# Self attention of a decoder layer: score matmuls of two heads in the two halves of the array's rows, units of eight heads, row sums on VectorE, and all loops written out

## The chip, the cores and the metric

The kernel runs on one core of a Trainium2 chip. The metric is the device time of one launch in microseconds. Engines are named as in the profile: PE is TensorE (PEld its weight loads), DVE is VectorE, ACT is ScalarE, POOL is GpSimd, SP is the queue that issues most DMAs.

## The reference

One decoder layer on x of 32 batches x 128 tokens x 128 channels. Only its first part matters for the change:

```python
xn = layernorm(layernorm(x), ln_w, ln_b)
q, k, v = (einsum('bsd,hde->bshe', xn, W) + b for W, b in ...)   # 16 heads of 64
scores = einsum('bqhe,bkhe->bhqk', q, k) / 8, causal mask
z = einsum('bhqk,bkhe->bqhe', softmax(scores), v)
x = x + einsum('bqhe,hed->bqd', z, W_o) + b_o
x = x + cross_attention(layernorm(x), context)                  # 16 heads of 8
x = x + mixture_of_experts(layernorm(x))                        # 8 experts, top 2
```

## The kernel before

The kernel has three stages, one after the other: self attention over the 32 batches, cross attention over the 32 batches, and the experts over eight groups of four batches. The last two batches of self attention are interleaved with the beginning of cross attention (`run_joined`). Each engine has a program of its own, in which the order of the work is written out by hand, and engines meet only in semaphores. An engine takes its instructions strictly in the order written.

**Units and steps.** In self attention `body(b, parity, valid, steps)` is one batch, and its four steps g = 0..3 (`G1`) each begin the scores of one unit of four heads (`HPG`). Work of several batches is in flight: in the body of batch b, step g holds the scores of unit g of batch b, the transposes of unit g-2, the products with the values (z) of unit g-3 (both may belong to batch b-1; `back` works that out), the output projection of batch b-1 (step 3), the Q, K and V projections of batch b+1 (steps 0, 1, 2) and the layer norm of batch b+2.

**One unit.** PE writes the causal mask into a bank of `ps` (a 128x512 matmul with `ident_b`) and adds the scores of four heads. For this `qz` holds the queries of each head over all 128 rows, with zeros in the 64 rows that belong to the other head of the pair, so that every score matmul uses the whole array. DVE takes the row maxima (L640). ACT makes the exponentials, 128 columns at a time because each head has its own bias, and has each instruction give the row sum too (`accum_out`, L536). DVE inverts the sums (L646), POOL multiplies `probs` by them (L390), PE transposes the four blocks (L994), ACT copies the bank to `probsT` (L531), PE multiplies by the values in two halves of the array's columns, and ACT copies that to `zT` (L526). Scores use banks 0 and 1 in turn, transposes banks 2 and 3, z bank 6, projections banks 4 and 5, and bank 7 serves the layer norm's transpose and the output.

**The other work of DVE in a body.** Step 0: queries from the bank to `qz` (L657, four instructions of 64 partitions, two halves of the projection by two heads of a pair) and statistics of the first norm (L681, L684). Step 1: keys to `kT` (L662, two instructions), the first norm (L675) and statistics of the second. Step 2: the second norm `xn` (L687), which waits for POOL's `rstd` (L400). Step 3: `xT` from the bank (L634) and the residual (L693). Matmuls that go through the helper `mm` all bear line 944.

**Loops.** `run_batches` writes out the first bodies, up to batch 2, loops over two bodies at a time (`Fori`), and writes out the last ones. Cross attention does the same, the experts loop over their groups.

Of the kernel before, what the change touches and what calls it, by code (L numbers as in the profile page):

```python
# [19 lines left out]
ALU = mybir.AluOpType  # L20
# [3 lines left out]
P = 128  # L24
# [7 lines left out]
E2 = D // H  # L32
G2 = 8
# [40 lines left out]
def run_batches(eng, first, last, body, steps, after={}):  # L74

    for b in range(first, 3):  # L80
        peel(body, b, steps)
        if b in after:
            after[b]()
    with eng.Fori(3, NB - 3, 2) as i:
        body(i, 1, lambda k: True, steps)
        body(i + 1, 0, lambda k: True, steps)
    for b in range(NB - 3, last):
        peel(body, b, steps)
# [17 lines left out]
def build(nc, x, ctx, W_q, W_k, W_v, W_o, b_q, b_k, b_v, b_o, ln_w, ln_b, w_qkv, w_proj, b_proj,  # L106
          gate_w, gate_proj_w, up_proj_w, down_proj_w, out):
    es = ExitStack()
    with es:
# [51 lines left out]
        qz = sb("qz", [P, 2, PAIRS, 2, P])  # L161
# [55 lines left out]
        raw_gu = qz[:, :, :, :, :].rearrange("p a t c q -> p (a t c) q")  # L217
# [18 lines left out]
        q_rows_zeroed = sem("q_rows_zeroed"); values_zeroed = sem("values_zeroed")  # L236
# [16 lines left out]
        sa_inverse_sums = sem("sa_inverse_sums")  # L253
# [46 lines left out]
        def _(sp):  # L300
# [25 lines left out]
            sp.wait_ge(sa_z_in_bank, G1 * NB)  # L326
# [11 lines left out]
            with sp.Fori(1, NC) as c:  # L338

                sp.wait_ge(expert_added, NE * c + NE)  # L340
                sp.dma_start(out_r[:, bass.ds(CB * c, CB), :], x_all[:, bass.ds(CB * c, CB), :]).then_inc(stored, 16)
# [3 lines left out]
        def _(pool):  # L345
# [154 lines left out]
            with pool.Fori(1, NC) as c:  # L500
                experts(c, False)
# [3 lines left out]
        def _(act):  # L505
# [12 lines left out]
            def self_attention(b, parity, valid, steps):  # L518
                for g in steps:
                    off, u, _ = back(b, parity, g, 3, G1)  # L520
                    if valid(off):
                        t = G1 * (b + off) + u
                        act.wait_ge(sa_z_in_bank, t + 1)
                        if u == 0 and valid(off - 1):
                            act.wait_ge(sa_output, b + off)
                        nc.scalar.copy(zT[:, 2 * u:2 * u + 2, :], ps[6][:, 0:2 * P]).then_inc(sa_z_taken, 1)  # L526
                    off, u, _ = back(b, parity, g, 2, G1)
                    if valid(off):
                        t = G1 * (b + off) + u
                        act.wait_ge(sa_pT_in_bank, t + 1)  # L530
                        nc.scalar.copy(probsT[:, u % 2, :], ps[2 + u % 2][:, :]).then_inc(sa_pT_taken, 1)  # L531
                    if valid(0):
                        t = G1 * b + g
                        act.wait_ge(sa_max, t + 1)
                        for i in range(HPG):
                            last = nc.scalar.activation(probs[:, g, i * P:(i + 1) * P],  # L536
                                                        ps[g % 2][:, i * P:(i + 1) * P], ACT.Exp,
                                                        bias=nmax[:, g, i:i + 1],
                                                        accum_out=rsum[:, g, i:i + 1])
                        last.then_inc(sa_exp, 1)  # L540
                    if g == 2 and valid(1):
# [74 lines left out]
            with act.Fori(1, NC) as c:  # L616
                experts(c, False)
# [3 lines left out]
        def _(dve):  # L621
            nc.vector.memset(qz[:, :, :, :, :], 0.0).then_inc(q_rows_zeroed, 1)

# [4 lines left out]
            def self_attention(b, parity, valid, steps):  # L628
                for g in steps:
# [7 lines left out]
                    if valid(0):  # L637
                        t = G1 * b + g
                        dve.wait_ge(sa_scores, t + 1)
                        nc.vector.reduce_max(nmax[:, g, :], ps[g % 2][:, :].rearrange("p (h k) -> p h k", h=HPG),  # L640
                                             AX_X, negate=True).then_inc(sa_max, 1)
                    off, u, _ = back(b, parity, g, 1, G1)
                    if valid(off):
                        t = G1 * (b + off) + u
                        dve.wait_ge(sa_exp, t + 1)
                        nc.vector.reciprocal(rinv[:, u, :], rsum[:, u, :]).then_inc(sa_inverse_sums, 1)  # L646

                    if valid(1) and g < 2:
                        n, np_ = b + 1, (parity + 1) % 2
                        for half in range(2):  # L650
# [3 lines left out]
                            if g == 0:  # L654
                                for a in range(2):
                                    r = slice(64 * a, 64 * a + 64)
                                    last = nc.vector.scalar_tensor_tensor(  # L657
                                        out=qz[r, np_, own, a, :], in0=tiles[r],
                                        scalar=E1 ** -0.5 / (X1_SCALE * W_SCALE), in1=bcast(bq[r, own], P),
                                        op0=ALU.mult, op1=ALU.add)  # L660
# [35 lines left out]
            def prepare():  # L696
# [6 lines left out]
                dve.wait_ge(q_rows_zeroed, 1)  # L703
# [232 lines left out]
            with dve.Fori(1, NC) as c:  # L936
                experts(c, False)
# [4 lines left out]
        def _(pe):  # L942
# [3 lines left out]
            def self_attention(b, parity, valid, steps):  # L946
                for g in steps:
# [5 lines left out]
                    if g == 2 and valid(0) and not valid(-1):  # L953

                        pe.wait_ge(raw_s_taken, 3)
                        pe.wait_ge(quad_weights_ready, 8)
                        pe.wait_ge(bo_ready, 1)
                    if valid(0):

                        t = G1 * b + g  # L960
                        if g == 0:
                            pe.wait_ge(sa_qk_taken, 4 * b + 4)
                        if g >= 2 or valid(-1):
                            pe.wait_ge(sa_exp, t - 1)
                        bank = ps[g % 2]
                        mm(bank[:, :], ident_b[:, :], causal[:, :, :].rearrange("p h k -> p (h k)"), True, False)
                        for i in range(HPG):
                            h = HPG * g + i
                            last = mm(bank[:, i * P:(i + 1) * P], qz[:, parity, h // 2, h % 2, :],
                                      kT[:, parity, h // 2, :], False, i == HPG - 1)  # L970
# [299 lines left out]
```

## Time and profile before

| | us |
|---|---|
| median of 3 runs | 1299.23 |
| lowest, highest | 1298.95, 1302.72 |
| profiled execution, span from first to last instruction | 1296.2 |
| self attention, first to last causal mask on PE | 26.94 to 531.75 |
| cross attention alone, about | 544 to 1000 |
| experts, about | 1030 to 1296 |

The page gives for the profiled execution its span alone, 1296.2 us; the time of a run also holds what lies before the first and after the last instruction, so the two differ by 3.0 us. Over the whole span PE is busy for 94%, DVE 74%, ACT 69%, POOL 35%. The stages have different limits, so these shares have to be read by stretch: within self attention PE shows 94.6%, DVE 62%, ACT 64%. A body of self attention takes 16.1 us in the trace.

### The profile page before, as it was taken

To read this page: it belongs to the slowest core of one execution; us is meant where nothing else is said; L and a number is where in the kernel's file an instruction comes from. 1 tells how busy PE (TensorE), PEld (TensorE's weight loads), DVE (VectorE), ACT (ScalarE), POOL (GpSimd) and SP (SyncE) were. 2 spreads that over 40 slices of the span, in tenths; PEclk is the share of its full clock that TensorE was granted. 3 is DMA by queue.
4 is the path that set the end of the run, shared out by engine and by line. 5 is a ranking of instruction groups with operands and counts; after the bars stand their busy time and mean duration, and the time that the engine had idled before them with its cause. 6 is when DMAs were issued, how large, how long until landed. Compare 5 with 4: busy or idle time off the path is not lost.

```text
span 1296.2 us, 35573 instructions
## 1 busy us (share of the span) xinstructions
PE 1218.0 (94%) x11851; PEld 932.5 (72%) x11851; DVE 954.3 (74%) x2179; ACT 895.0 (69%) x2950; POOL 448.7 (35%) x796
## 2 busy tenths in 40 slices
PE   5999999999999999899999999999998699999997
PEld 3788888888888778777777777777776366665565
DVE  6666666666666665488888888888886778888887
ACT  2666666666666666698888888888886465555554
POOL 3444444444444444322323333232331342222222
PEclk9999999999999999999999999999999799999999
DMA  6000000000000000000000000000030000000000
GB/s 151 2 2 0 0 0 0 0 0 0 0 0 0 0 0 2 5 14 10 8 12 8 8 11 10 8 8 12 8 102 2 1 10 9 8 8 8 8 8 9
DMA packets 20558, 14.59 MB, mean 11 GB/s; under 512 B 7042, under 2 KB 18596, under 8 KB 20516
## 3 DMA queue, kind: packets, MB, share of 16 engines
q1 hardware_dynamic: 20176, 13.90, 3.9%
q8 instruction: 25, 0.41, 0.1%
q10 hardware_dynamic: 340, 0.14, 0.0%
q14 instruction: 17, 0.14, 0.0%
HBM read 11.94 MB, written 2.10 MB: 11 GB/s over the span
## 4 chain that ended last, share of the span: by engine, by line
PE 47%; issue 23%; DVE 20%; ACT 5%; POOL 3%; DVEq 1%; DMA 1%; POOLq 0%; SPq 0%; ACTq 0%
PE ps L944 35%; PE ps L1088 6%; DVE qz L657 4%; ACT probs L563 3%; PE ps L994 3%; DVE kT L662 3%; DVE xn L687 2%; DVE nmax L785 2%; DVE bst L681 1%; POOL rstd L400 1%; DVE x_all L910 1%; DVE wk L923 1%; POOL h_lo L494 1%; DMA wv<-in_L_attn_W_v 1%; PE ps L952 1%
## 5 line engine op out<-in xcount | busy, mean ns | idle before, releaser
L563 ACT ACTIVATE probs<-ps,nmax 128x256 f32<-128x256 f32 x512 | 238.7, 477 | 13.3 <-DVE nmax L785 11.3
L536 ACT ACTIVATE probs<-ps,nmax 128x128 f32<-128x128 f32 x512 | 183.3, 385 | 28.2 <-DVE nmax L640 28.0
L785 DVE TENSOR_REDUCE nmax<-ps 128x2 f32<-128x512 f32 x256 | 175.3, 685 | 35.3 <-PE ps L944 34.5
L390 POOL TENSOR_TENSOR probs<-probs,rinv 128x512 f32<-128x512 f32 x128 | 133.1, 1040 | 124.7 <-DVE rinv L646 124.7
L944 PE MATMUL ps<-probsT,vm 128*32 128x128 f32 x2048 | 161.5, 279 | 0.0
L1088 PE MATMUL ps<-ident,probs 128*128 128x128 f32 x1024 | 154.5, 273 | 1.2 <-ACT probs L563 1.1
L554 ACT COPY probsT<-ps 128x512 f32<-128x512 f32 x224 | 131.9, 589 | 28.5 <-PE ps L1088 28.1
L526 ACT COPY zT<-ps 128x256 f32<-128x256 f32 x128 | 48.6, 380 | 147.3 <-PE ps L944 147.1
L494 POOL TENSOR_TENSOR h_lo<-wk,h_hi 128x512 f16<-128x512 f32 x64 | 74.0, 1156 | 189.0 <-ACT h_hi L611 186.1
L944 PEld LDWEIGHTS ps<-kT,qz 128*128 128x128 f32 x1024 | 134.5, 192 | 4.0
L944 PE MATMUL ps<-kT,qz 128*128 128x128 f32 x1024 | 134.9, 275 | 0.0
L603 ACT ACTIVATE wq<-ps 128x512 f32<-128x512 f32 x128 | 76.6, 598 | 72.6 <-PE ps L944 72.4
L640 DVE TENSOR_REDUCE nmax<-ps 128x4 f32<-128x512 f32 x128 | 88.3, 690 | 48.0 <-PE ps L944 46.9
L944 PEld LDWEIGHTS ps<-probsT,vm 128*32 128x32 f32 x2048 | 92.8, 109 | 42.7 <-issue 42.5
L1088 PEld LDWEIGHTS ps<-ident,probs 128*128 128x128 f32 x1024 | 118.4, 141 | 7.1 <-ACT probs L563 2.1
L536 ACT ACTIVATION_READ_ACCUMULATOR probs<-ps,nmax 128x1 f32 x512 | 114.3, 223 | 0.0
L928 DVE TENSOR_TENSOR h_lo<-wk,h_hi 128x512 f16<-128x512 f32 x64 | 76.0, 1188 | 43.8 <-ACT h_hi L611 43.8
L611 ACT CAST h_hi<-wk 128x512 f16<-128x512 f32 x128 | 74.3, 617 | 48.7 <-PE ps L944 32.0
L563 ACT ACTIVATION_READ_ACCUMULATOR probs<-ps,nmax 128x1 f32 x512 | 105.3, 206 | 0.0
L944 PE MATMUL ps<-kT,qm 128*128 128x256 f16 x512 | 98.5, 274 | 6.4 <-ACT probs L563 4.3
L944 PE MATMUL ps<-xnT_hi,w_hi 128*128 (+1 forms) x256 | 99.1, 387 | 4.2 <-DVE wk L923 2.4
L657 DVE SCALAR_TENSOR_TENSOR qz<-ps,bq 64x512 f32<-64x512 f32 x128 | 88.1, 688 | 15.4 <-PE ps L944 13.6
(196 smaller groups left out, 3048.7 us busy)
## 6 DMA issues: line engine op xcount, KB each, us to landing
ctx_row<-in_ctx SPq DMA_DIRECT2D x32, 128.0 KB, 2.1
out_x<-x_all SPq DMA_DIRECT2D x8, 256.0 KB, 2.3
kT<-in_L_ffn_down_proj_w SPq DMA_DIRECT2D x1, 1024.0 KB, 10.8
wq<-in_L_attn_W_q SPq DMA_DIRECT2D x1, 512.0 KB, 5.0
wk<-in_L_attn_W_k SPq DMA_DIRECT2D x1, 512.0 KB, 10.1
wv<-in_L_attn_W_v SPq DMA_DIRECT2D x1, 512.0 KB, 10.4
wo<-in_L_attn_W_o SPq DMA_DIRECT2D x2, 256.0 KB, 6.0
x_all<-in_x SPq DMA_DIRECT2D x1, 256.0 KB, 3.0
```

Source lines behind the costliest of these rows:

```text
L390: nc.gpsimd.tensor_tensor(pr, pr, bcast(rinv[:, u, :], P), ALU.mult).then_inc(sa_probs, 1)
L494: nc.gpsimd.tensor_tensor(h_lo[:, e % 2, 0, :], hT[:, 0, :], h_hi[:, e % 2, 0, :], ALU.subtract).then_inc(hidden_low_first, 1)
L536: last = nc.scalar.activation(probs[:, g, i * P:(i + 1) * P], ps[g % 2][:, i * P:(i + 1) * P], ACT.Exp, bias=nmax[:, g, i:i + 1], accum_ou ...
L554: nc.scalar.copy(probsT[:, u % 4, :], ps[2 + u % 2][:, :]).then_inc(ca_pT_taken_act, 1)
L563: last = nc.scalar.activation(probs[:, g % 4, i * KEYS2:(i + 1) * KEYS2], ps[SCORE_BANKS2[g]][:, i * KEYS2:(i + 1) * KEYS2], ACT.Exp, bias ...
L603: nc.scalar.activation(silu[:, i, :], ps[i][:, :], ACT.Silu, scale=1.0 / (NORM_SCALE * W_SCALE)).then_inc(silu_ready, 1)
L640: nc.vector.reduce_max(nmax[:, g, :], ps[g % 2][:, :].rearrange("p (h k) -> p h k", h=HPG), AX_X, negate=True).then_inc(sa_max, 1)
L657: last = nc.vector.scalar_tensor_tensor(out=qz[r, np_, own, a, :], in0=tiles[r], scalar=E1 ** -0.5 / (X1_SCALE * W_SCALE), in1=bcast(bq[r, ...
L785: nc.vector.reduce_max(nmax[:, g, 0:2], ps[SCORE_BANKS2[g]][:, :].rearrange("p (h k) -> p h k", h=2), AX_X, negate=True).then_inc(ca_max, 1)
L928: nc.vector.tensor_tensor(h_lo[:, e % 2, 1, :], hT[:, 1, :], h_hi[:, e % 2, 1, :], ALU.subtract).then_inc(hidden_low_second, 1)
L944: return nc.tensor.matmul(o, l, r, start=start, stop=stop, **kw)
L1088: last = nc.tensor.transpose(ps[2 + u % 2][:, i * P:(i + 1) * P], probs[:, u % 4, i * P:(i + 1) * P], ident[:, :])
```

## The change

It does the following, in self attention except where stated:

- The queries are no longer spread over `qz` with zeros. `qT` holds a pair of heads over 128 partitions, as `kT` does, and is written by two DVE instructions of 128 partitions instead of four of 64. The memset of `qz` goes.
- A score matmul uses the 64 rows of its head, for queries and keys. The two heads of a pair go to the two halves of the array's rows and to two different banks. PE issues the scores of eight heads at once (`HALVES`), in step 0 into banks 0 and 1 and in step 1 into banks 2 and 3, with two mask matmuls ahead of each.
- The softmax units stay at four heads (even or odd ones of eight). Their exponentials no longer give row sums. DVE adds up each unit's `probs` (`reduce_sum`, 128x512 in SBUF), waits for its own semaphore, and inverts.
- z of batch b-1 is made in step 2 of batch b, two halves of eight heads one after the other, in banks 0 and 1, after the exponentials of units 0 and 1 of batch b have read them. ACT copies each half (128x512) to `zT` after the exponentials of unit 2, and after these it takes the transposes of unit 0.
- All transposes go to bank 6, so each unit's transposes wait for ACT's copy of the one before. `probsT` has four buffers in use.
- All `Fori` loops, of cross attention and of the experts too, are written out.

The diff, with the removed loops of the other engines and the declarations left out:

```diff
@@ -81,10 +82,7 @@
-    with eng.Fori(3, NB - 3, 2) as i:
-        body(i, 1, lambda k: True, steps)
-        body(i + 1, 0, lambda k: True, steps)
-    for b in range(NB - 3, last):
+    for b in range(3, last):
...
@@ -158,7 +156,8 @@
-        qz = sb("qz", [P, 2, PAIRS, 2, P])
+        raw_gu = sb("raw_gu", [P, 2 * NE * HT, P])
+        qT = raw_gu[:, 0:2 * PAIRS, :].rearrange("p (a t) q -> p a t q", a=2)
...
@@ -335,10 +333,10 @@
-            with sp.Fori(1, NC) as c:
+            for c in range(1, NC):
-                sp.dma_start(out_r[:, bass.ds(CB * c, CB), :], x_all[:, bass.ds(CB * c, CB), :]).then_inc(stored, 16)
+                sp.dma_start(out_r[:, CB * c:CB * c + CB, :], x_all[:, CB * c:CB * c + CB, :]).then_inc(stored, 16)
...
@@ -516,28 +514,31 @@
                 nc.scalar.activation(w1_hi[:, i, :, :], w[:, :, :], ACT.Copy, scale=W_SCALE).then_inc(w1_high_ready, 1)
 
             def self_attention(b, parity, valid, steps):
-                for g in steps:
-                    off, u, _ = back(b, parity, g, 3, G1)
-                    if valid(off):
-                        t = G1 * (b + off) + u
-                        act.wait_ge(sa_z_in_bank, t + 1)
-                        if u == 0 and valid(off - 1):
-                            act.wait_ge(sa_output, b + off)
-                        nc.scalar.copy(zT[:, 2 * u:2 * u + 2, :], ps[6][:, 0:2 * P]).then_inc(sa_z_taken, 1)
+                def copy_transposed(g):
                     off, u, _ = back(b, parity, g, 2, G1)
                     if valid(off):
-                        t = G1 * (b + off) + u
-                        act.wait_ge(sa_pT_in_bank, t + 1)
-                        nc.scalar.copy(probsT[:, u % 2, :], ps[2 + u % 2][:, :]).then_inc(sa_pT_taken, 1)
+                        act.wait_ge(sa_pT_in_bank, G1 * (b + off) + u + 1)
+                        nc.scalar.copy(probsT[:, u, :], ps[6][:, :]).then_inc(sa_pT_taken, 1)
+
+                for g in steps:
+                    if g != 2:
+                        copy_transposed(g)
                     if valid(0):
-                        t = G1 * b + g
-                        act.wait_ge(sa_max, t + 1)
+                        act.wait_ge(sa_max, G1 * b + g + 1)
                         for i in range(HPG):
                             last = nc.scalar.activation(probs[:, g, i * P:(i + 1) * P],
-                                                        ps[g % 2][:, i * P:(i + 1) * P], ACT.Exp,
-                                                        bias=nmax[:, g, i:i + 1],
-                                                        accum_out=rsum[:, g, i:i + 1])
+                                                        ps[g][:, i * P:(i + 1) * P], ACT.Exp,
+                                                        bias=nmax[:, g, i:i + 1])
                         last.then_inc(sa_exp, 1)
+                    if g == 2 and valid(-1):
+                        n = b - 1
+                        if valid(-2):
+                            act.wait_ge(sa_output, n)
+                        for half in range(HALVES):
+                            act.wait_ge(sa_z_in_bank, HALVES * n + half + 1)
+                            nc.scalar.copy(zT[:, 4 * half:4 * half + 4, :], ps[half][:, :]).then_inc(sa_z_taken, 1)
+                    if g == 2:
+                        copy_transposed(g)
                     if g == 2 and valid(1):
                         n, np_ = b + 1, (parity + 1) % 2
                         for half in range(2):
...
@@ -635,14 +634,16 @@
                                                 ALU.mult, ALU.add).then_inc(sa_xT_taken, 1)
 
                     if valid(0):
-                        t = G1 * b + g
-                        dve.wait_ge(sa_scores, t + 1)
-                        nc.vector.reduce_max(nmax[:, g, :], ps[g % 2][:, :].rearrange("p (h k) -> p h k", h=HPG),
+                        dve.wait_ge(sa_scores, HALVES * b + g // 2 + 1)
+                        nc.vector.reduce_max(nmax[:, g, :], ps[g][:, :].rearrange("p (h k) -> p h k", h=HPG),
                                              AX_X, negate=True).then_inc(sa_max, 1)
                     off, u, _ = back(b, parity, g, 1, G1)
                     if valid(off):
                         t = G1 * (b + off) + u
                         dve.wait_ge(sa_exp, t + 1)
+                        nc.vector.reduce_sum(rsum[:, u, :], probs[:, u, :].rearrange("p (h k) -> p h k", h=HPG),
+                                             AX_X).then_inc(sa_sums, 1)
+                        dve.wait_ge(sa_sums, t + 1)
                         nc.vector.reciprocal(rinv[:, u, :], rsum[:, u, :]).then_inc(sa_inverse_sums, 1)
 
                     if valid(1) and g < 2:
...
@@ -652,12 +653,10 @@
-                                for a in range(2):
-                                    r = slice(64 * a, 64 * a + 64)
-                                    last = nc.vector.scalar_tensor_tensor(
-                                        out=qz[r, np_, own, a, :], in0=tiles[r],
-                                        scalar=E1 ** -0.5 / (X1_SCALE * W_SCALE), in1=bcast(bq[r, own], P),
-                                        op0=ALU.mult, op1=ALU.add)
+                                last = nc.vector.scalar_tensor_tensor(
+                                    out=qT[:, np_, own, :], in0=tiles,
+                                    scalar=E1 ** -0.5 / (X1_SCALE * W_SCALE), in1=bcast(bq[:, own], P),
+                                    op0=ALU.mult, op1=ALU.add)
...
@@ -950,53 +948,54 @@
                         if valid(-2):
                             pe.wait_ge(sa_residual, b - 1)
                         nc.tensor.transpose(ps[7][:, 0:P], xn[:, :], ident[:, :]).then_inc(sa_xT_in_bank, 1)
-                    if g == 2 and valid(0) and not valid(-1):
-
-                        pe.wait_ge(raw_s_taken, 3)
-                        pe.wait_ge(quad_weights_ready, 8)
-                        pe.wait_ge(bo_ready, 1)
-                    if valid(0):
-
-                        t = G1 * b + g
+                    if valid(0) and g < HALVES:
+
                         if g == 0:
                             pe.wait_ge(sa_qk_taken, 4 * b + 4)
-                        if g >= 2 or valid(-1):
-                            pe.wait_ge(sa_exp, t - 1)
-                        bank = ps[g % 2]
-                        mm(bank[:, :], ident_b[:, :], causal[:, :, :].rearrange("p h k -> p (h k)"), True, False)
+                        if g == 1 and not valid(-1):
+                            pe.wait_ge(raw_s_taken, 3)
+                            pe.wait_ge(quad_weights_ready, 8)
+                            pe.wait_ge(bo_ready, 1)
+                        if valid(-1):
+                            pe.wait_ge(sa_exp, G1 * (b - 1) + 2 * g + 2)
+                        for a in range(2):
+                            mm(ps[2 * g + a][:, :], ident_b[:, :], causal[:, :, :].rearrange("p h k -> p (h k)"),
+                               True, False)
                         for i in range(HPG):
-                            h = HPG * g + i
-                            last = mm(bank[:, i * P:(i + 1) * P], qz[:, parity, h // 2, h % 2, :],
-                                      kT[:, parity, h // 2, :], False, i == HPG - 1)
+                            for a in range(2):
+                                r = slice(E1 * a, E1 * a + E1)
+                                last = mm(ps[2 * g + a][:, i * P:(i + 1) * P], qT[r, parity, HPG * g + i, :],
+                                          kT[r, parity, HPG * g + i, :], False, i == HPG - 1)
                         last.then_inc(sa_scores, 1)
-                    off, u, par = back(b, parity, g, 3, G1)
-                    if valid(off):
-
-                        t = G1 * (b + off) + u
-                        pe.wait_ge(sa_pT_taken, t + 1)
-                        if u == 0:
-                            pe.wait_ge(sa_v_taken, 2 * (b + off) + 2)
-                        if u > 0 or valid(off - 1):
-                            pe.wait_ge(sa_z_taken, t)
-                        for i in range(HPG):
-                            h = HPG * u + i
-                            a = h % 2
-                            last = mm(ps[6][64 * a:64 * a + 64, (i // 2) * P:(i // 2 + 1) * P],
-                                      v1[:, par, h * E1:(h + 1) * E1], probsT[:, u % 2, i * P:(i + 1) * P])
-                        last.then_inc(sa_z_in_bank, 1)
+                    if g == 2 and valid(-1):
+
+                        n, before = b - 1, (parity + 1) % 2
+                        for half in range(HALVES):
+                            pe.wait_ge(sa_pT_taken, G1 * n + 2 * half + 2)
+                            if half == 0:
+                                pe.wait_ge(sa_v_taken, 2 * n + 2)
+                            if valid(0):
+                                pe.wait_ge(sa_exp, G1 * b + half + 1)
+                            for i in range(HPG):
+                                for a in range(2):
+                                    h = 2 * (HPG * half + i) + a
+                                    last = mm(ps[half][64 * a:64 * a + 64, i * P:(i + 1) * P],
+                                              v1[:, before, h * E1:(h + 1) * E1],
+                                              probsT[:, 2 * half + a, i * P:(i + 1) * P])
+                            last.then_inc(sa_z_in_bank, 1)
                     off, u, par = back(b, parity, g, 2, G1)
                     if valid(off):
                         t = G1 * (b + off) + u
                         pe.wait_ge(sa_probs, t + 1)
-                        if u >= 2 or valid(off - 1):
-                            pe.wait_ge(sa_pT_taken, t - 1)
+                        if t > 0:
+                            pe.wait_ge(sa_pT_taken, t)
                         for i in range(HPG):
-                            last = nc.tensor.transpose(ps[2 + u % 2][:, i * P:(i + 1) * P],
+                            last = nc.tensor.transpose(ps[6][:, i * P:(i + 1) * P],
                                                        probs[:, u, i * P:(i + 1) * P], ident[:, :])
                         last.then_inc(sa_pT_in_bank, 1)
                     if g == 3 and valid(-1):
                         n = b - 1
-                        pe.wait_ge(sa_z_taken, G1 * n + G1)
+                        pe.wait_ge(sa_z_taken, HALVES * n + HALVES)
                         if valid(2):
                             pe.wait_ge(sa_xT_taken, b + 3)
                         if not valid(0):
```

## Rows read from the trace of the kernel before

**Rows 1.** The page: its head, the fetches of instructions, and one table line of DMA issues.

```profile
span 1296.2 us, 35573 instructions
...
q8 instruction: 25, 0.41, 0.1%
...
ctx_row<-in_ctx SPq DMA_DIRECT2D x32, 128.0 KB, 2.1
```

**Rows 2.** Busy time in one body: PE, PEld, DVE, ACT, POOL (instructions), clock, DMA.

```profile
300.36:316.45 16.09, 15.22 (x158) 12.94 (x156) 10.00 (x22) 10.25 (x43) 6.81 (x11) 1.00 0.00 0
```

**Rows 3.** Timeline of PE in one body: start, us taken, instruction; projections between them left out.

```profile
301.70 0.38 PE L944 MATMUL ps<-causal,ident_b 128*128 128x512 bf16 x1
301.92 1.05 PE L944 MATMUL ps<-kT,qz 128*128 128x128 f32 x8
302.90 0.66 PE L944 MATMUL ps<-probsT,v 128*64 128x128 f32 x8
303.49 0.66 PE L994 MATMUL ps<-ident,probs 128*128 128x128 f32 x4
...
305.33 0.38 PE L944 MATMUL ps<-causal,ident_b 128*128 128x512 bf16 x1
...
309.93 0.33 PE L952 MATMUL ps<-ident,xn 128*128 128x128 f32 x1 [0.86 <-DVE xn L687]
310.10 0.38 PE L944 MATMUL ps<-causal,ident_b 128*128 128x512 bf16 x1
...
311.88 0.66 PE L994 MATMUL ps<-ident,probs 128*128 128x128 f32 x4
312.38 1.95 PE L944 MATMUL ps<-wo,zT 128*128 128x128 f32 x16
314.16 0.38 PE L944 MATMUL ps<-causal,ident_b 128*128 128x512 bf16 x1
```

**Rows 4.** Timeline of DVE in the same body and the next.

```profile
311.40 0.69 DVE L640 TENSOR_REDUCE nmax<-ps 128x4 f32<-128x512 f32 x1 [0.69 <-PE ps L944]
...
317.32 2.81 DVE L657 SCALAR_TENSOR_TENSOR qz<-ps,bq 64x512 f32<-64x512 f32 x4 [0.43 <-PE ps L944]
320.16 0.29 DVE L681 BATCH_NORM_STATS2 bst<-x_all 128x6 f32 x1
320.61 0.18 DVE L684 BATCH_NORM_AGGREGATE mv<-bst 128x2 f32<-128x6 f32 x1 [0.15 <-DVE bst L681]
320.82 0.69 DVE L640 TENSOR_REDUCE nmax<-ps 128x4 f32<-128x512 f32 x1
321.43 0.17 DVE L646 RECIPROCAL rinv<-rsum 128x4 f32<-128x4 f32 x1
321.51 1.26 DVE L662 SCALAR_TENSOR_TENSOR kT<-ps,bk 128x512 f32<-128x512 f32 x2
...
323.72 0.69 DVE L640 TENSOR_REDUCE nmax<-ps 128x4 f32<-128x512 f32 x1
...
324.91 1.05 DVE L687 TENSOR_SCALAR xn<-zln,mv,rstd 128x128 f32<-128x128 f32 x1 [0.41 <-POOL rstd L400]
```

**Rows 5.** Timeline of ACT, a copy of transposes and the first exponential of a unit.

```profile
316.80 0.64 ACT L531 COPY probsT<-ps 128x512 f32<-128x512 f32 x1
317.27 0.43 ACT L536 ACTIVATE probs<-ps,nmax 128x128 f32<-128x128 f32 x1
317.53 0.26 ACT L536 ACTIVATION_READ_ACCUMULATOR probs<-ps,nmax 128x1 f32 x1
```

**Rows 6.** Timeline of POOL: the multiply of one unit.

```profile
324.84 1.04 POOL L390 TENSOR_TENSOR probs<-probs,rinv 128x512 f32<-128x512 f32 x1
```

**Rows 7.** Timeline of DVE: the same instruction in two bodies written out, and in a loop.

```profile
67.24 1.05 DVE L687 TENSOR_SCALAR xn<-zln,mv,rstd 128x128 f32<-128x128 f32 x1 [0.45 <-POOL rstd L400]
...
83.36 1.05 DVE L687 TENSOR_SCALAR xn<-zln,mv,rstd 128x128 f32<-128x128 f32 x1 [0.41 <-POOL rstd L400]
...
308.82 1.05 DVE L687 TENSOR_SCALAR xn<-zln,mv,rstd 128x128 f32<-128x128 f32 x1 [0.41 <-POOL rstd L400]
```

More of the change, by code:

```diff
@@ L32 @@
 E2 = D // H
+HALVES = 2
 G2 = 8
@@ L215, in build @@
         h_lo = sb("h_lo", [P, 2, HT, CB * P], F16)
-        raw_gu = qz[:, :, :, :, :].rearrange("p a t c q -> p (a t c) q")
         bv_wide = probsT[:, 0:2, :].rearrange("p a q -> p (a q)")
@@ L235, in build @@
         ln_ready = sem("ln_ready"); biases_transposed = sem("biases_transposed")
-        q_rows_zeroed = sem("q_rows_zeroed"); values_zeroed = sem("values_zeroed")
+        values_zeroed = sem("values_zeroed")
         w1_high_ready = sem("w1_high_ready"); w1_low_ready = sem("w1_low_ready")
@@ L252, in build @@
         sa_scores = sem("sa_scores"); sa_max = sem("sa_max"); sa_exp = sem("sa_exp")
-        sa_inverse_sums = sem("sa_inverse_sums")
+        sa_sums = sem("sa_sums"); sa_inverse_sums = sem("sa_inverse_sums")
         sa_probs = sem("sa_probs"); sa_pT_in_bank = sem("sa_pT_in_bank"); sa_pT_taken = sem("sa_pT_taken")
@@ L324, in _ @@
             run_batches(sp, -1, NB - 1, context, None)
-            sp.wait_ge(sa_z_in_bank, G1 * NB)
+            sp.wait_ge(sa_z_in_bank, HALVES * NB)
             tiles = NE * HT
@@ L499, in _ @@
             experts(0, True)
-            with pool.Fori(1, NC) as c:
+            for c in range(1, NC):
                 experts(c, False)
@@ L615, in _ @@
             experts(0, True)
-            with act.Fori(1, NC) as c:
+            for c in range(1, NC):
                 experts(c, False)
@@ L621, in _ @@
         def _(dve):
-            nc.vector.memset(qz[:, :, :, :, :], 0.0).then_inc(q_rows_zeroed, 1)
             dve.wait_ge(ln_transposed, 1)
@@ L702, in prepare @@
                 dve.wait_ge(biases_ready, 1)
-                dve.wait_ge(q_rows_zeroed, 1)
                 for i, w in enumerate((wq, wk, wv)):
@@ L935, in _ @@
             experts(0, True)
-            with dve.Fori(1, NC) as c:
+            for c in range(1, NC):
                 experts(c, False)
@@ L1172, in _ @@
             pe.wait_ge(sa_residual, NB)
-            pe.wait_ge(sa_z_taken, G1 * NB)
+            pe.wait_ge(sa_z_taken, HALVES * NB)
             run_batches(pe, 0, NB + 2, cross_attention, range(G2))
@@ L1220, in experts @@
             def experts(c, first):
-                own = slice(0, CB) if first else bass.ds(CB * c, CB)
+                own = slice(CB * c, CB * c + CB)
                 rows_hi = xnT_hi[:, own, :].rearrange("p b t -> p (b t)")
@@ L1244, in _ @@
             experts(0, True)
-            with pe.Fori(1, NC) as c:
+            for c in range(1, NC):
                 experts(c, False)
```

## The prediction

> **What bounds the kernel now.** I read the busy time by stretch first, then the timelines of PE, DVE, ACT and POOL over one body of self attention. In a body of 16.09 us PE is busy for 15.22 and no other engine for more than 10.3 [rows 2], at the full clock (1.00, 2.4 GHz). PE's pieces, start to start, say what the time is made of [rows 3]: a mask 0.22, the scores of four heads 0.98, z of four heads 0.59, four transposes 0.50, a projection of Q or K 1.34 (303.49 to 305.33 less the transposes), V 1.30 (six matmuls of 512 columns like the mask's, at 0.216), the norm's transpose 0.17, the output 1.78. One body: 4 x (0.22 + 0.98 + 0.59 + 0.50) + 2 x 1.34 + 1.30 + 0.17 + 1.78 = 15.09. The last us is a wait for DVE's `xn`, 0.86 of it shown as idle [rows 3]. So PE sets the pace, with DVE's chain 1 us longer than PE's work at one place.
>
> From the first mask to the last there are 504.8 us (table), 31.4 such bodies; the first and the last are shorter, so about 30 periods run at this pace. Cross attention and the experts keep their instructions.
>
> **PE's part of the change.** The 16 output records take 1.78, 0.11 each; scores run at the same pace (8 x 0.11 = 0.88, and 0.10 where z begins). z, whose pairs use the two halves of the columns, needs 0.59 for as many records: 0.055 each and 0.15 for the change from whole to split array and back [rows 3]. Row halves don't occur in the trace. Bounds: 0.055 a record (both halves at once, as z's columns) and 0.11 (nothing gained). z is the nearest row, and I take 0.055. Scores of eight heads, S: two masks 0.43, 16 records 0.88, changes 0.25: 1.56, where it was 2.40. z of eight heads twice in a row, Z: 0.15 + 32 x 0.055 + 0.10 = 2.01, where it was 2.36. PE's work in a body falls to 2 x 1.56 + 2.01 + 4 x 0.50 + 2.68 + 1.30 + 0.17 + 1.78 = 13.06, 2.0 less. With PE's wait gone as well, 13.06 would be the period; the dependences below forbid it.
>
> The Trainium skill, "TensorEngine Tiling (Array Packing)", Key Properties, has different tiles execute weight loads and matmuls in parallel, which would make 0.055 right. "TensorE: Matmul & The Clock Gate", section LDWEIGHTS, speaks against the change: a load costs by its columns, and a low one as much as a full one. z's loads have 64 columns, these 128; if two loads queued, a pair would take 0.22 as before and the sum would be that of the second rival.
>
> **DVE's part.** Two query instructions go, each 0.71 (2.84 for four [rows 4]): -1.42. Four sums come. Their nearest row is the maxima of the same shape, 0.69 long and 0.61 to the next start. The wait for the own semaphore adds what lies between statistics and their aggregation, 0.16 [rows 4]; so 0.85 from sum to reciprocal, four times 3.4. DVE's work rises from 10.0 to 12.0 [rows 2], still under the period, but it lies in one chain.
>
> **ACT's part.** An exponential starts a read of its sum after 0.26 and the read 0.09 later the next; without the read I take 0.26 a head, 1.04 a unit. The bound above is the instruction's own length, 0.43 [rows 5]. A copy of 512 columns takes 0.47 to the next start, 0.60 to its end.
>
> **One body, step by step.** t = 0 is the first mask of S0 in batch b. PE: S0 to 1.56, transposes of unit 2 of b-1 to 2.06, Q to 3.40, S1 to 4.96, transposes of unit 3 to 5.46, K to 6.80, Z to 8.81, transposes of unit 0 to 9.31, V to 10.61. Then it needs `xn`, the multiplied unit 1 and the free bank 6.
>
> DVE: before, the maxima started at 311.40, 0.11 after the scores gave way to z (311.88 - 0.59) [rows 3, 4]. Now at 1.67. Sum of unit 3 of b-1 2.28, reciprocal 3.13, queries 3.21, statistics 4.63, maxima of unit 1 5.29 (0.66 later, as 320.16 to 320.82), sum of unit 0 5.90, reciprocal 6.75, keys 6.83, maxima of unit 2 9.04 (2.21 for keys and first norm, 321.51 to 323.72), sum of unit 1 9.65, reciprocal 10.50, `xn` 10.58 [rows 4]. `xn` took 1.05 while POOL's multiply, begun 0.07 earlier, ran for 1.04 [rows 4, 6]; now it starts first. If it still collides it ends at 11.7, which costs nothing.
>
> POOL multiplies unit 1 from 10.74 to 11.78. But the exponentials of unit 2 begin at 9.76 (maxima 0.69, 0.03 to ACT) and end at 10.80. Behind them on ACT stand the two copies of z, 0.47 each, then the copy of unit 0's transposes to 12.34. Only then is bank 6 free: what is late is this copy. Transposes of unit 1 from 12.39, output from 12.89, next S0 at 14.67. Queued behind PE's wait for bank 6 are these transposes, the output and all next scores.
>
> All other waits are met: z's second half needs the copy of unit 3 and the exponentials of unit 1, both over by 7.2; the multiplied units 3, 0 and 2 are there before their transposes. So the period is 14.67 for 16.10, 1.43 less: 30 x 1.43 = 42.9. Two query instructions less before the first scores, where the load of W_v holds up the preparation and DVE then does them: 1.4. The memset ran under that load: 0. The last body ends with two halves instead of four small steps and a sum more; I estimate the ends at -0.5 together, bounds +2 and -3 (a sum and a longer copy more, periods shorter by 1.4 less).
>
> **Loops.** Two bodies written out lie 16.12 apart, two in the loop 16.09 (308.82 to 324.91) [rows 4, 7]: no cost of a loop's turn. I take 1 us off for some twenty turns in all stages, bounds 0 and -3.
>
> Sum: 1296.2 - 42.9 - 1.4 - 0.5 - 1.0 = 1250.4 for the span. The median is 3.0 above the span of the profiled execution; 1253.4 against 1299.23.
>
> Own range: exponentials at 0.43 a head add 0.68 to the period (15.35, 1274); the sum's gap gone and ends at their best take 0.3 (14.4, 1245).
>
> **Rivals.**
> - *Loads of the two row halves queue.* Each S costs 0.88 more. Maxima of unit 0 shift by 0.88, and K ends at 8.56, so that the second key tile comes 0.4 later than DVE asks for it: 14.67 + 0.88 + 0.4 = 15.95. 30 x 0.15 + 1.4 + 1: 1292 to 1296, say 1295, half of it within 0.3% (3.9 us, about what a measurement tells from no change). For it: no row has two loads of 128 columns at once. Against: z's pairs.
> - *Sums held up by POOL, slower than before.* `xn` shows that DVE can stand still for a whole multiply [rows 4, 6]. Three sums lie on the way to unit 1's transposes (11.83, slack 0.56): with d more each, the period grows by 3d - 0.56. From d = 0.66 the gain is gone; at a full 1.04 it is 17.2, 1299.2 + 30 x 1.13 - 2 = 1331. Against: a multiply starts 0.24 after its reciprocal and the next sum at least 2.7 after it, so they don't meet, unless every sum is slow by itself.
> - *Fetching written-out code.* Before, the page counts 25 fetches, 16 KB each [rows 1], for a program whose bodies were mostly looped. All written out, about a third of it was there, so some 55 more. They cost nothing in the bodies written out so far [rows 7]. If each stopped PE for the landing time of a context load, 2.1 us [rows 1], they would cost 115: 1369. It decides from 0.8 us a fetch. The skill's "Advanced Engine Details and Errata", ISA Cache, has just two lines of 256 instructions, so straight code is always fetched anew; that is this rival, and no row bears it out.
> - *PE's work alone sets the period*: 13.06, 1296.2 - 30 x 3.04 + 3 = 1207. It needs ACT's order not to matter; the copies of z stand there.
>
> **Chances.** Forecast 0.72; queued loads 0.10 (half of it no change); sums held up 0.05; fetches 0.06; PE's work alone, or anything near it, 0.03; the rest 0.04 between. Faster by over 0.3% 0.82, within 0.06, slower 0.12. For 8 in 10 I widen the own range to 1238 to 1286, towards queued loads above and a shorter chain below.
>
> **What the profile would show.** Score records in pairs, 16 in 0.88 after two masks; one body 14.7; PE idle from about 10.6 to 12.4 but for the norm's transpose, released by ACT's copy; `reduce_sum` at 0.69; no read of accumulators; exponentials 0.26 apart; `xn` at 0.35. Wrong if scores take 1.8, if exponentials keep 0.35, or if PE idles without a releaser where code is fetched.

## Result and profile after

The changed kernel takes 1242.67 us (median of 4, 1240.6 to 1243.82) where the kernel before takes 1299.15: ratio 0.9556, 95% interval 0.9538 to 0.9573. The forecast was 1253, its range 1238 to 1286.

The page of the changed kernel: the span and the two queues that fetch instructions.

```profile
span 1241.3 us, 31536 instructions
...
q8 instruction: 96, 1.57, 0.5%
q14 instruction: 54, 0.44, 0.1%
```

The span is 54.9 us shorter. By marks that both traces have: until the first mask 1.1 (26.9, now 25.9); from there to the first scores of cross attention alone 47.2 (517.7, now 470.5); cross attention 1.8; routing 0.1; first to last silu of the experts 3.4 (269.6, now 266.2); after the last silu 1.4. So 6.7 us came from stages of which only the loops were changed. The start up to the first mask is not settled by one execution: it ends between 26.8 and 28.9 us in the profiled kernels that leave the preparation as it was.

Of self attention the steady part gained more than the 47.2: 1.70 a body over some 30 bodies is 51.0. The rest was lost where self attention ends. There the granted clock of PE fell to its lower level (1.2 GHz). Busy time in that stretch (PE, PEld, DVE, ACT, POOL, then the clock), and PE's pieces in it:

```profile
486.80:496.00 9.20, 8.49 (x52) 7.49 (x52) 0.00 (x0) 1.76 (x3) 0.00 (x0) 0.50 0.00 0
```

```profile
486.83 1.11 PE L993 MATMUL ps<-ident,probs 128*128 128x128 f32 x4 [2.25 <-POOL probs L388]
487.87 3.68 PE L942 MATMUL ps<-probsT,v 128*64 128x128 f32 x32
492.24 3.78 PE L942 MATMUL ps<-wo,zT 128*128 128x128 f32 x16 [0.68 <-ACT zT L539]
```

The three pieces take 0.63, 1.97 and 1.95 at the full clock, so the lower level cost 4.0 us. The kernel before has the full clock (1.00) in the same place, and its last output takes 2.05.

PE's timeline over one body of the changed kernel, the masks, projections and the norm's transpose left out:

```profile
300.72 1.16 PE L942 MATMUL ps<-kT,raw_gu 64*128 64x128 f32 x16
301.81 0.66 PE L993 MATMUL ps<-ident,probs 128*128 128x128 f32 x4
...
303.74 1.97 PE L942 MATMUL ps<-probsT,v 128*64 128x128 f32 x32
305.64 0.66 PE L993 MATMUL ps<-ident,probs 128*128 128x128 f32 x4
...
308.90 0.63 PE L993 MATMUL ps<-ident,probs 128*128 128x128 f32 x4 [1.20 <-ACT probsT L521]
309.37 1.95 PE L942 MATMUL ps<-wo,zT 128*128 128x128 f32 x16
...
323.77 1.95 PE L942 MATMUL ps<-wo,zT 128*128 128x128 f32 x16
```

From output to output a body takes 14.40 us, where it was 16.1 [rows 4, 7]. Scores of eight heads begin in 300.72 and give way in 301.81: 1.09 for 16 records, where four heads alone took 0.98 [rows 3]. z of 16 heads takes 1.90. PE stands 1.20 us ahead of the transposes of unit 1, released by ACT's copy to `probsT`.

DVE in the next body, then ACT in the first:

```profile
312.89 0.69 DVE L638 TENSOR_REDUCE nmax<-ps 128x4 f32<-128x512 f32 x1 [1.24 <-PE ps L942]
313.50 0.68 DVE L644 TENSOR_REDUCE rsum<-probs 128x4 f32<-128x512 f32 x1
314.21 0.18 DVE L647 RECIPROCAL rinv<-rsum 128x4 f32<-128x4 f32 x1
314.30 1.26 DVE L656 SCALAR_TENSOR_TENSOR raw_gu<-ps,bq 128x512 f32<-128x512 f32 x2
315.48 0.28 DVE L680 BATCH_NORM_STATS2 bst<-x_all 128x6 f32<-128x128 f32 x1
```

```profile
306.17 1.14 ACT L529 ACTIVATE probs<-ps,nmax 128x128 f32<-128x128 f32 x4 [2.04 <-DVE nmax L638]
307.18 1.09 ACT L539 COPY zT<-ps 128x512 f32<-128x512 f32 x2
308.12 0.64 ACT L521 COPY probsT<-ps 128x512 f32<-128x512 f32 x1
```

A sum costs 0.71 to its reciprocal (313.50 to 314.21), two query instructions 1.18 (314.30 to 315.48). The four exponentials of a unit take 1.14, 0.25 apart. Behind them come the copies of z and then the one that PE waits for. The chain of the same stretch in order of time says what is late:

```profile
302.47 0.68 PE ps L942 x12
...
303.18 1.36 DVE kT L661 x2
...
305.56 0.59 DVE nmax L638
...
306.43 0.88 ACT probs L529 x3
307.31 0.96 ACT zT L539 x2
308.27 0.50 ACT probsT L521
...
308.90 0.63 PE ps L993 x4
```

It enters DVE at the keys from PE's K projection (x12, its first half), and not from the sums. The margin is small: DVE's reciprocal at 302.88 takes 0.18, and the keys begin at 303.18.

### The profile page after: what moved, and what is told of

Its sections match the earlier page's. It is cut to its first block, busy times and chain, and to the rows that moved or that the text cites. A ratio compares the mean times of both kernels' runs of the same rounds, so it can differ in the third digit from the quotient of the medians.

```text
span 1241.3 us, 31536 instructions
## 1 busy us (share of the span) xinstructions
PE 1153.1 (93%) x11818; PEld 869.5 (70%) x11851; DVE 943.1 (76%) x2242; ACT 834.6 (67%) x2374; POOL 453.6 (37%) x796
## 4 chain that ended last, share of the span: by engine, by line
PE 52%; issue 16%; ACT 16%; DVE 10%; POOL 6%; DMA 1%; SPq 0%; DVEq 0%; POOLq 0%
PE ps L942 38%; PE ps L1087 7%; ACT probs L564 5%; POOL h_lo L492 5%; PE ps L993 5%; DVE kT L661 3%; ACT probsT L555 3%; ACT zT L539 2%; ACT probs L529 2%; DVE nmax L638 2%; ACT probsT L521 1%; ACT k_hi L559 1%; DVE bst L680 1%; DMA wv<-in_L_attn_W_v 1%; PE ps L1120 1%
## 5 line engine op out<-in xcount | busy, mean ns | idle before, releaser
L783 DVE TENSOR_REDUCE nmax<-ps 128x2 f32<-128x512 f32 x256 | 176.3, 689 | 48.2 <-PE ps L942 45.0
L529 ACT ACTIVATE probs<-ps,nmax 128x128 f32<-128x128 f32 x512 | 148.4, 390 | 72.4 <-DVE nmax L638 72.4
L521 ACT COPY probsT<-ps 128x512 f32<-128x512 f32 x128 | 78.4, 612 | 127.4 <-PE ps L993 127.4
L555 ACT COPY probsT<-ps 128x512 f32<-128x512 f32 x224 | 131.9, 589 | 34.8 <-PE ps L1087 32.6
L1087 PE MATMUL ps<-ident,probs 128*128 128x128 f32 x1024 | 153.8, 273 | 1.2 <-ACT probs L564 1.1
L1087 PEld LDWEIGHTS ps<-ident,probs 128*128 128x128 f32 x1024 | 119.6, 141 | 5.0 <-ACT probs L564 2.1
L993 PE MATMUL ps<-ident,probs 128*128 128x128 f32 x512 | 83.6, 286 | 41.3 <-ACT probsT L521 37.1
L564 ACT ACTIVATION_READ_ACCUMULATOR probs<-ps,nmax 128x1 f32 x512 | 105.8, 207 | 0.0
L612 ACT CAST h_hi<-wk 128x512 f16<-128x512 f32 x128 | 77.9, 617 | 40.9 <-DVE wk L921 40.8
L926 DVE TENSOR_TENSOR h_lo<-wk,h_hi 128x512 f16<-128x512 f32 x64 | 71.8, 1123 | 43.8 <-ACT h_hi L612 43.8
L942 PE MATMUL ps<-xnT_hi,w_hi 128*128 128x512 f16 x256 | 99.6, 389 | 2.7 <-DVE wk L921 2.7
L942 PE MATMUL ps<-xnT_lo,w_hi 128*128 128x512 f16 x256 | 98.9, 386 | 0.0
L993 PEld LDWEIGHTS ps<-ident,probs 128*128 128x128 f32 x512 | 54.0, 141 | 63.8 <-POOL probs L388 50.7
L942 PE MATMUL ps<-xnT_hi,w_lo 128*128 128x512 f16 x256 | 98.6, 385 | 0.0
```

The lines of the kernel that those rows point to most:

```text
L521: nc.scalar.copy(probsT[:, u, :], ps[6][:, :]).then_inc(sa_pT_taken, 1)
L555: nc.scalar.copy(probsT[:, u % 4, :], ps[2 + u % 2][:, :]).then_inc(ca_pT_taken_act, 1)
L564: last = nc.scalar.activation(probs[:, g % 4, i * KEYS2:(i + 1) * KEYS2], ps[SCORE_BANKS2[g]][:, i * KEYS2:(i + 1) * KEYS2], ACT.Exp, bias ...
L612: nc.scalar.copy(h_hi[:, e % 2, i, :], hT[:, i, :]).then_inc(hidden_high, 1)
L783: nc.vector.reduce_max(nmax[:, g, 0:2], ps[SCORE_BANKS2[g]][:, :].rearrange("p (h k) -> p h k", h=2), AX_X, negate=True).then_inc(ca_max, 1)
L942: return nc.tensor.matmul(o, l, r, start=start, stop=stop, **kw)
```

## Experiments

Bodies are taken from the starts of `xn` in steady stretches. All ratios are to the kernel before.

**Row halves one after the other.**

```diff
-for i in range(HPG):
-    for a in range(2):
+for a in range(2):
+    for i in range(HPG):
         r = slice(E1 * a, E1 * a + E1)
```

> The changed kernel with the order of the two heads of a pair swapped: first the four heads of one row half, then the four of the other. Theory A (matmuls and weight loads of the two halves run at once only when they stand next to each other): scores of eight heads take about 0.9 us more, K ends 1.8 us later and the body takes 16.1 us, near 1294 us. Rival (the halves give nothing, the gain is the new order of units): no change, 1242 us.

1278.13 us, 0.9837 (0.9820 to 0.9854). PE's timeline:

```profile
302.20 1.95 PE L942 MATMUL ps<-wo,zT 128*128 128x128 f32 x16
...
304.51 1.71 PE L942 MATMUL ps<-kT,raw_gu 64*128 64x128 f32 x16
306.15 0.66 PE L993 MATMUL ps<-ident,probs 128*128 128x128 f32 x4
...
317.70 1.95 PE L942 MATMUL ps<-wo,zT 128*128 128x128 f32 x16
```

A body takes 15.50. The scores take 1.64 for 1.09, and 2 x 0.55 is the 1.1 us that the body grows by; 32 bodies give 35 us, the measured difference. The rival falls: the order of the records alone is worth 35 of the change's 56.5 us, so the new order of units is not the whole gain. Theory A has the direction right and the size too large, 0.55 for 0.9: in this order the second half's first record starts while the last three of the first half are still to come (single records of the second half start at 305.07, 305.28, 305.39, those of the first end with 305.06, 305.17, 305.29, 305.40). PE overlaps the halves even when they don't alternate, a few records deep. A kernel whose halves never overlap was not run; from 16 records at 0.11, S would take 0.88 more and the body 1.76, 56 us in all. That is an estimate.

**Row sums by ScalarE again.**

```diff
 nc.scalar.activation(probs[...], ps[g][...], ACT.Exp,
-                     bias=nmax[:, g, i:i + 1])
+                     bias=nmax[:, g, i:i + 1],
+                     accum_out=rsum[:, g, i:i + 1])
...
-nc.vector.reduce_sum(rsum[:, u, :], probs[:, u, :]..., AX_X).then_inc(sa_sums, 1)
-dve.wait_ge(sa_sums, t + 1)
```

> The changed kernel with the row sums given by ScalarE's exponentials again (accum_out) and no reduce_sum on VectorE. Theory A (the chain of VectorE with its sums sets the period, as predicted): two sums of 0.71 us leave the way to the maxima of unit 2, a body takes about 13.3 to 13.6 us for 14.4, near 1212 us. Theory B (TensorE's K projection releases the keys just as late, and behind it ScalarE's exponentials of unit 2 stand in the way): the maxima stay where they are, the exponentials start 0.35 us apart for 0.25, a body takes 14.8, near 1254 us.

1252.31 us, 0.9635 (0.9619 to 0.9650): 9.6 us slower than the change. A body takes 14.78. Its chain of waits, in order of time:

```profile
309.73 1.36 DVE kT L659 x2
...
312.99 1.25 ACT probs L529 x7
314.23 0.96 ACT zT L540 x2
```

The keys are still released by PE; from them to the copies of z it is now 4.50 us, where it was 4.13 (303.18 to 307.31). With no sum on DVE nothing is gained there, and the reads of the accumulators cost 0.37 a body on ACT. Theory B holds. (`xn` takes 1.05 here, as before the change, but ACT's copy still ends last.)

**Each sum twice.**

```diff
+nc.vector.reduce_sum(rsum[:, 4 + u, :], probs[:, u, :]..., AX_X)
 nc.vector.reduce_sum(rsum[:, u, :], probs[:, u, :]..., AX_X).then_inc(sa_sums, 1)
```

> The changed kernel with each reduce_sum issued twice (the first into unused columns). Theory A (two sums stand on VectorE's way to the keys, with 0.2 us to spare): 2 x 0.6 - 0.2 = 1.0 us more a body, 15.4 us, near 1274 us. Rival (the sums lie beside the projection of K with more to spare): under 0.3 us a body more, below 1252 us.

1300.25 us (1293.94 to 1306.98), 1.0003 (0.9979 to 1.0027): much slower than either theory. There are two kinds of bodies. Busy time by stretch (PE, PEld, DVE, ACT, POOL, then PE's granted clock), and PE's output projection in one body of each stretch:

```profile
110.00:160.00 50.00, 44.39 (x457) 36.64 (x454) 36.11 (x82) 24.85 (x72) 20.32 (x32) 0.90 0.01 2
...
260.00:310.00 50.00, 44.38 (x529) 36.44 (x528) 40.67 (x94) 26.72 (x77) 22.47 (x36) 1.00 0.01 2
```

```profile
149.69 0.33 PE L952 MATMUL ps<-ident,xn 128*128 128x128 f32 x1 [1.12 <-DVE xn L688]
150.78 0.63 PE L995 MATMUL ps<-ident,probs 128*128 128x128 f32 x4 [0.76 <-ACT probsT L521]
151.24 3.50 PE L944 MATMUL ps<-wo,zT 128*128 128x128 f32 x16
```

```profile
281.85 0.33 PE L952 MATMUL ps<-ident,xn 128*128 128x128 f32 x1 [1.12 <-DVE xn L688]
282.94 0.63 PE L995 MATMUL ps<-ident,probs 128*128 128x128 f32 x4 [0.76 <-ACT probsT L521]
283.40 1.95 PE L944 MATMUL ps<-wo,zT 128*128 128x128 f32 x16
```

At the clock of 1.00 a body takes 15.29, 0.88 more than the changed kernel, near theory A's 1.0: of the 1.2 us of two more sums 0.3 were free. So the sums lie beside the K projection with little to spare. Where the clock averages 0.90, it drops to its lower level (1.2 GHz) once a body, after the two waits of PE, and the output takes 3.50 for 1.95; such a body takes 16.9. In the profiled execution, the slowest of the ten, 21 of 31 bodies are of this kind. They cost 34 us by the clock, and the sums 0.88 a body, 27 us: together some 62 of the 64 us between the two spans. The same waits, 1.12 and 0.76, stand before both. What decides between them is not shown.

**Copies ahead of the exponentials.** In step 2 of ScalarE's program:

```diff
 for g in steps:
-    if g != 2:
-        copy_transposed(g)
+    if g == 2 and valid(-1):
+        ...                    # the two copies of z, with their waits
+    copy_transposed(g)
     if valid(0):
         ...                    # exponentials of unit g
-    if g == 2 and valid(-1):
-        ...
-    if g == 2:
-        copy_transposed(g)
```

> The changed kernel, on ScalarE in step 2 the two copies of z and the copy of unit 0's transposes stand ahead of the exponentials of unit 2. Theory A (bank 6 waits for ScalarE's order): TensorE's idle 1.2 us shrinks until unit 1's multiply by GpSimd ends, a body takes 13.7 us, near 1222 us. Rival (the wait is for the multiply of unit 1 or for the norm): 14.4 us, 1242 us.

1217.31 us, 0.9371 (0.9350 to 0.9393), 25.4 us less than the change. A body takes 13.66. On PE:

```profile
309.08 0.66 PE L990 MATMUL ps<-ident,probs 128*128 128x128 f32 x4 [0.42 <-POOL probs L388]
```

PE's wait is 0.42 and its releaser is now POOL's multiply. Theory A holds, with its number. This version beats both kernels.

**Both edits on ScalarE.**

> The changed kernel with both edits on ScalarE: the copies of z and of unit 0's transposes ahead of the exponentials of unit 2, and the row sums by accum_out. Theory A (with the copies out of the way the exponentials' length is hidden, and the sum of unit 1 on VectorE is what is left before the multiply): a body falls to TensorE's own work, 13.2 us, near 1207 us. Rival (longer exponentials or the norm hold TensorE up as in the run with sums alone): 13.7 us or more, 1217 us or more.

1219.86 us, 0.9389 (0.9366 to 0.9411); a body takes 13.82, where the order alone gives 13.66. Theory A fell, and the rival's 13.7 or more holds. The whole times of the two runs lie too close to tell them apart; the bodies do. Its chain, and PE's output:

```profile
308.62 0.58 POOL rstd L398
309.23 1.06 DVE xn L681
310.34 0.34 PE ps L945
310.71 0.42 DVE xT L631
```

```profile
311.26 2.02 PE L937 MATMUL ps<-wo,zT 128*128 128x128 f32 x16 [0.16 <-DVE xT L631]
```

Without the sum of unit 1 DVE reaches its reciprocal before POOL has made `rstd`. POOL goes on from `rstd` straight to the multiply (309.16), and `xn` collides with it again: 1.06 us, as before the change [rows 4], where it is 0.32 in the changed kernel. The output, which waits until `xT` has been read, is late. With the sum on DVE the multiply starts only after `xn` has (307.02 and 306.86 in the changed kernel). That is read from this trace; moving `xn` ahead of the reciprocal was not tried.

**The kernel before with all loops written out.**

> The kernel before with all loops written out and nothing else. Theory A (the traces' 0.58 us a group of experts and 0.07 us a turn of cross attention are the loops'): 7 to 9 us less than before, near 1291 us. Theory B (my prediction's price): 1 us less. Rival (fetching more code costs time): slower.

1291.80 us, 0.9943 (0.9929 to 0.9958), 7.4 us less. A group of experts takes 32.53 for 33.12 and a body of self attention 16.07 where it alternated between 16.08 and 16.13. Theory A holds, and the rival falls, though the page counts as many fetches as with the whole change:

```profile
q8 instruction: 97, 1.59, 0.5%
...
q14 instruction: 58, 0.48, 0.1%
```

**One engine's expert loop at a time.** In each run `with engine.Fori(1, NC) as c` becomes `for c in range(1, NC)` for one engine, in the kernel before.

> The kernel before with only TensorE's loop over the groups of experts written out, so that its waits and addresses there are constants; all other loops stay. Theory A (the 0.58 us a group is TensorE's, whose waits on a computed value come late between two experts): the groups take 32.5 us for 33.1, 5 us less in all, near 1294 us. Rival (it is VectorE's or GpSimd's loop): no change, 1299 us.

> The kernel before with only VectorE's loop over the groups of experts written out. Theory A (TensorE's loop costs the time): no change, 1299 us, groups of 33.1 us. Rival: groups of 32.5 us, near 1294 us.

> The kernel before with only ScalarE's loop over the groups of experts written out. Theory A (ScalarE's waits on computed values let each first copy to h_hi start 0.07 us late, 0.78 us after VectorE's product begins where the written-out kernel has 0.71, and GpSimd and VectorE follow it): groups of 32.6 us for 33.1, 4 to 5 us less in all, near 1294.5 us. Rival (it takes several engines' loops together): 33.1 us, 1299 us.

> The kernel before with only GpSimd's loop over the groups of experts written out. Theory A (it is ScalarE's loop): no change, 1299 us, groups of 33.1 us. Rival (GpSimd's waits): groups of 32.6 us, near 1294.5 us.

| loop written out | us | ratio, interval | a group |
|---|---|---|---|
| none (kernel before) | 1299.16 and 1299.56 | | 33.12 |
| TensorE | 1299.03 | 1.0003, 0.9991 to 1.0015 | 33.1 |
| VectorE | 1299.91 | 1.0003, 0.9993 to 1.0014 | 33.13 |
| ScalarE | 1296.89 | 0.9975, 0.9966 to 0.9984 | 32.61 |
| GpSimd | 1298.37 | 0.9993, 0.9982 to 1.0004 | 33.06 |

My first theory, TensorE's loop, fell. It is ScalarE's, 0.51 a group, and GpSimd's 0.06 by the trace alone (its time can't be told from the kernel before); together they are 0.57 of the 0.59. With ScalarE's loop out the groups take what was expected, but the whole fell by 2.7 us and not by 4 to 5. The profiled execution offers a reason: at the end of self attention, whose program that run leaves as it was, its clock fell to 0.51 (540.1 to 544.1 us) and the last output took 3.27 for 2.05. In the kernel before, VectorE's product for the experts and the copy that waits for it:

```profile
1099.64 1.27 DVE L923 SCALAR_TENSOR_TENSOR wk<-ps,wq 128x512 f32<-128x512 f32 x2
...
1100.42 1.14 ACT L611 CAST h_hi<-wk 128x512 f16<-128x512 f32 x2 [0.72 <-PE ps L944]
...
1101.12 1.16 POOL L494 TENSOR_TENSOR h_lo<-wk,h_hi 128x512 f16<-128x512 f32 x1 [2.98 <-ACT h_hi L611]
1101.60 1.23 DVE L928 TENSOR_TENSOR h_lo<-wk,h_hi 128x512 f16<-128x512 f32 x1 [0.68 <-ACT h_hi L611]
```

With ScalarE's loop alone written out:

```profile
1099.35 1.27 DVE L923 SCALAR_TENSOR_TENSOR wk<-ps,wq 128x512 f32<-128x512 f32 x2
...
1100.06 1.22 ACT L611 CAST h_hi<-wk 128x512 f16<-128x512 f32 x2 [0.73 <-DVE wk L923]
1100.75 1.16 POOL L494 TENSOR_TENSOR h_lo<-wk,h_hi 128x512 f16<-128x512 f32 x1 [2.91 <-ACT h_hi L611]
1101.30 1.15 DVE L928 TENSOR_TENSOR h_lo<-wk,h_hi 128x512 f16<-128x512 f32 x1 [0.69 <-ACT h_hi L611]
```

The copy starts 0.71 after the product for 0.78. POOL's subtraction starts 1.40 after the product for 1.48, and DVE's own, which ends with POOL's, ends 3.10 after it for 3.19. That this ring of DVE, ACT and POOL, and not PE alone, sets the pace of an expert is read from these starts, not tested by itself; 0.51 a group is 0.064 an expert.

## Why the prediction was right, and where it was off

**Scores at z's pace: right.** From the first mask to the next transposes S0 takes 1.62 (296.75 to 298.36), forecast 1.56. The rival with queued weight loads fell: it wanted 0.88 more. The Trainium skill's "TensorEngine Tiling (Array Packing)", Key Properties, has different tiles execute weight loads and matmuls in parallel. The trace agrees: 16 loads and 16 matmuls of scores lie within 1.1 us.

**The last step, ACT's order: right.** "What is late is this copy" is the 1.20 us in front of the transposes, and moving the copies brought 0.75 a body. Predicted was 12.39 for the transposes' start, measured 12.15 (308.90, with S0's first mask at 296.75, which is 0.22 before the second at 296.96; its own record is missing).

**The way there: right in length, wrong in what carries it.** I counted the sums of units 3 and 0 on DVE as part of the chain that sets the maxima of unit 2. They fill time in which DVE would otherwise wait for PE's K projection, with 0.3 to spare. Taking all sums away leaves the way from the keys on as it was; doubling them costs 0.88 of 1.2. The step had two sizes wrong as well: sum to reciprocal 0.71 for 0.85 (the wait for the own semaphore adds 0.03 after a sum, and not the 0.16 after statistics), and two query instructions 1.18 for 1.42, since a pair of 128 partitions takes what the keys take. A body came to 14.40 for 14.67: over 30 bodies 8.1 us better than forecast.

**The ends: mis-sized, and outside their bounds.** I put them at -0.5 (bounds +2 and -3) and gave the clock no term. They came to about +3.9, as much as the lower clock at the end of self attention cost (4.0). That is 4.4 us worse than forecast; the start, 1.1 for 1.4, is 0.3 worse. So self attention with its start came to 48.2 us less for 44.8, and that these lie only 3.4 apart is in part luck: 8.1 too little gain from the bodies, against 4.7 too much at the ends and the start.

**Loops: mis-sized.** I priced them at 1 us (bounds 0 and -3) from two bodies of self attention, where PE sets the pace and covers an engine's late wait. They are worth 6.7 us outside self attention, 7.4 in all by the run with nothing else changed. The term failed because it was read in one stage and used for three. These two balances, 3.4 and 5.7, make up the 9.1 us between the forecast span (1250.4) and the trace (1241.3). I added 3.0 from span to median; here it is 1.4, the other 1.6 of the 10.7 us.

**Rivals.** Sums held up by POOL: `reduce_sum` takes 0.67 to 0.68 in all 128 places. In the steady bodies it never runs beside POOL's multiply, so these do not test a collision; one near the end does, at 465.79, beside a multiply from 465.37 to 466.41, and takes 0.68 as well. Fetches: 71 more on the queue that I counted (I said 55), and 37 on the other; with 72 and 41 more the kernel before got 7.4 us faster, so whatever they cost is less than what the loops had cost. The Trainium skill's "Advanced Engine Details and Errata", ISA Cache, gives two lines of 256 instructions. That straight code is then fetched anew did not make it slower than the loops here. PE's work alone as the period (13.06) was not reached by any run; 13.66 was the best.

**Signs named ahead.** `xn` 0.32, exponentials 0.25 apart, no accumulator reads, PE idle until ACT's copy: all there. The ends and their clock had no sign named.

## What to carry to other kernels

When an engine's program is in order, ask which of its instructions another engine waits for, and put these ahead of work that nobody waits for yet: three copies moved up were worth nearly half of what the whole change brought (25.4 us beside 56.5). An instruction in a chain costs only what exceeds the other branch that meets it at the next step, so cost both branches before adding it up. Price an edit in each stage by the engine that sets that stage's pace; a late wait is free on one and counts in full on another. And compare a forecast with the trace term by term: here a span 9.1 us off hid a gain of the bodies 8.1 us too small and a loss at the ends 4.4 us too small.

## What the runs showed of the hardware that was not expected

- Matmuls on two halves of the array's rows overlap even when four of one half are issued before four of the other: 1.64 us for 16 records, where one at a time would be 1.97 by estimate (1.09 plus 8 x 0.11).
- In the run with doubled sums the clock dropped once a body in some stretches (mean 0.90, output projection 3.50 us for 1.95) and not in others (1.00), with the same waits of 1.12 and 0.76 us ahead of it. The changed kernel, with one wait of 1.20 in their place, kept 1.00 from 100 to 400 us, but fell to 0.50 from 486.8 to 496.0 us, after waits of 1.91, 0.39 and 2.25. What decides is not shown: the kernel before and the run with ScalarE's expert loop out have the same program there, and the first kept 1.00 where the second fell to 0.51.
- In ScalarE's loop over the groups, where the values of its waits are computed, a copy started 0.78 us after the product; written out, with constants, 0.71.
